# A kept-back stage prepared beside the last MLP, and an MLP bias on another engine

## What is computed

```python
# first block, B = 16 batches of 112 rows x 512 channels
out = attention(layer_norm(x, ln1), ctx) @ cproj_w + cproj_b
residual = out + x
y = gelu(layer_norm(residual, ln2) @ fc_w + fc_b, approximate=True) @ proj_w + proj_b
x = residual + y                                   # proj_b is the MLP bias
# second block: recurrence (time mixing), then channel mixing
x1 = x + group_norm(scan(r, k, v, w)) * g @ Wo.T
xc = _ln(x1, ln2_w, ln2_b)
sx2 = concatenate([state[:, 0:1] - xc[:, :1], xc[:, :-1] - xc[:, 1:]], axis=1)
xk2 = xc + sx2 * ffn_maa_k
xr2 = xc + sx2 * ffn_maa_r
rr = sigmoid(xr2 @ Wfr.T)
kk = square(relu(xk2 @ Wfk.T))
return x1 + rr * (kk @ Wfv.T)
```

## Time and profile before

| what | value |
|---|---|
| median of 3 executions | 1761.23 us (1757.83 to 1768.81) |
| the profiled execution | 1756.24 us, span 1753.9 us |
| PE busy | 1638.1 us (93%) |
| DVE busy | 1188.7 us (68%) |
| ACT busy | 657.4 us (37%) |
| POOL busy | 281.6 us (16%) |
| mean granted clock of TensorE | 0.975 |

### The profile page before, as it was taken

How to read it: one execution, slowest core, us unless ns; L and a number is a source line. 1 busy time by engine, 2 the same in 40 slices (tenths; PEclk the granted TensorE clock), 3 DMA queues, 4 the chain that set the end, 5 groups by cost and what they waited for, 6 DMA issues and landing times.

```text
span 1753.9 us, 21083 instructions
## 1 busy us (share of the span) xinstructions
PE 1638.1 (93%) x7912; PEld 855.8 (49%) x7912; DVE 1188.7 (68%) x1854; ACT 657.4 (37%) x1535; POOL 281.6 (16%) x377
## 2 busy tenths in 40 slices
PE   6999999799999999899999998999899898987968
PEld 3555544455555444455554445555444454433423
DVE  1233200367997995569988955799899576999741
ACT  2466420226664212246662222466431226212111
POOL 1100000123111001322110011221100132036020
PEclk9999999899999999999999999999999998999989
DMA  8001012143121124341112233510132343232221
GB/s 272 6 30 53 19 48 80 68 138 99 38 61 50 64 84 143 102 135 46 38 59 75 76 129 96 161 46 9 47 101 83 117 115 111 64 105 77 69 90 45
DMA packets 76914, 142.46 MB, mean 81 GB/s; under 512 B 16688, under 2 KB 26800, under 8 KB 76816
## 3 DMA queue, kind: packets, MB, share of 16 engines
q1 hardware_dynamic: 61664, 105.51, 18.9%
q0 software_dynamic: 11776, 31.70, 6.4%
q10 hardware_dynamic: 3376, 3.93, 0.7%
HBM read 117.26 MB, written 23.86 MB: 80 GB/s over the span
## 4 chain that ended last, share of the span: by engine, by line
PE 74%; DVE 16%; issue 4%; ACT 3%; ACTq 1%; DMA 1%; POOL 0%; DVEq 0%; POOLq 0%
PE bank L346 42%; PE bank L533 12%; PE bank L660 7%; PE bank L388 4%; DVE C L1399 3%; PE bank L380 3%; PE bank L400 2%; DVE sm L1336 1%; PE bank L626 1%; DVE C L1575 1%; DVE C L1391 1%; PE bank L611 1%; DVE SX L1399 1%; DVE C L1408 1%; DVE YB L1417 1%
## 5 line engine op out<-in xcount | busy, mean ns | idle before, releaser
L1399 DVE TENSOR_TENSOR_SCAN C<-XA,C 128x896 f32<-128x896 f32 x112 | 228.8, 2043 | 3.7 <-ACT XA L1091 0.5
L533 PE MATMUL bank<-ring,HT 128*112 128x512 f32 x512 | 222.3, 592 | 0.0
L1336 DVE CUSTOM_DVE_ANT_0 sm<-bank,maskb 112x375 f32<-112x375 f32 x256 | 124.3, 543 | 133.6 <-PE bank L380 133.1
L346 PE MATMUL bank<-ctx_t,Wk 128*128 128x375 f32 x512 | 195.2, 506 | 13.9 <-DMA Wk<-in_wk 12.5
L346 PE MATMUL bank<-SX,ring 128*128 128x448 f32 (+2 forms) x544 | 195.9, 519 | 4.1 <-issue 4.1
L346 PE MATMUL bank<-Wv,ctx_t 128*125 128x512 f32 x384 | 180.9, 596 | 0.4 <-ACT C L1057 0.4
L388 PEld LDWEIGHTS bank<-ident,sm 112*125 112x125 f32 x768 | 124.1, 190 | 105.6 <-ACT sm L1072 44.1
L1078 ACT ACTIVATE probT<-bank 125x336 f32<-125x336 f32 x256 | 114.3, 446 | 159.3 <-PE bank L388 157.6
L1072 ACT ACTIVATE sm<-sm,nm 112x375 f32<-112x375 f32 x256 | 153.4, 599 | 2.7 <-DVE nm L1336 2.7
L533 PEld LDWEIGHTS bank<-ring,HT 128*112 128x112 f32 x512 | 90.6, 177 | 127.2 <-issue 127.2
L346 PEld LDWEIGHTS bank<-SX,ring 128*128 128x128 f32 x544 | 100.5, 190 | 96.9 <-issue 94.0
(11 more groups left out here) (181 smaller groups left out, 2317.1 us busy)
## 6 DMA issues: line engine op xcount, KB each, us to landing
ring<-in_stream SPq DMA_DIRECT2D x64, 1024.0 KB, 5.4
ctx_t<-in_ctxT SPq DMA_DIRECT2D x16, 750.0 KB, 4.7
rkw_scratch<-HT POOLq DMA_DIRECT2D x32, 224.0 KB, 4.3
rkw<-rkw_scratch POOLq DMA_DIRECT2D x24, 224.0 KB, 3.1
HT<-in_x SPq DMA_DIRECT2D x16, 224.0 KB, 5.2
X<-in_x SPq DMA_DIRECT2D x16, 224.0 KB, 5.1
rkw_scratch<-YB POOLq DMA_DIRECT2D x16, 224.0 KB, 3.1
v_scratch<-HT POOLq DMA_DIRECT2D x16, 224.0 KB, 5.6
```

The source lines that it names most:

```text
L346: last_ = nc.tensor.matmul(out_ap, pairs[k][0], pairs[k][1], start=(k == 0), stop=(k == len(pairs) - 1))
L533: last_ = nc.tensor.matmul(bank[SC[b]][0:LQ, :], HT[:, c, b * LQ:(b + 1) * LQ], w[:, c, :], start=(m == 0 and c == 0), stop=(m == 3 and c ...
L1336: nc.vector.tensor_tensor_reduce(out=sm[0:LQ, slot, :], in0=tile(name)[0:LQ, 0:LK], in1=maskb[:, n % 2, :], scale=-SCALE, scalar=3.0e38, o ...
L1399: own.step(nc.vector.tensor_tensor_scan(out=part, data0=wrep[:, i % 2, :], data1=part, initial=0.0, op0=ALU.mult, op1=ALU.add))
```

## The change

Three things change.

1. `LAST` becomes 0, 2, 1, 3: stage 0 now handles group 0 and stage 1 handles group 2. Rows of groups 0 and 1 are both loaded from DRAM into `sm`.
2. The preparation of stage 0 moves from `pre(3)` into the last MLP: `last_stats(0)` behind the first whole iteration of the scan that runs there, `last_std(0)` on POOL at the same place, `last_norm(0)` on ACT one batch behind each GELU of quarter m = 0, the transposes between the first projection and the second FC, the columns behind the fourth normalisation, and `last_mixes(0)` between `group_norm` and `gate`. At the end of `pre(3)`, `last_mixes(1)` takes its place ahead of the last scan; on ACT and PE the columns of stage 1 stand between the second and the third tile of the gate product.
3. `mlp_bias` goes from DVE to POOL: four adds of one batch each, and `mlp_add` waits for them.

```diff
-LAST = [2, 0, 1, 3]
+LAST = [0, 2, 1, 3]
...
-            return x1_b[b] if LAST[k] == 0 else X[:, GB * (LAST[k] == NG - 1) + b, :]
+            return x1_b[b] if LAST[k] < 2 else X[:, GB * (LAST[k] == NG - 1) + b, :]
...  (tensor, mlp)
                     else:
                         piece_done(g, ("pj", m))
+                    if g == NG - 1 and m == 0:
+                        last_cols(0)
...  (tensor, pre)
-                if g == NG - 1:
-                    last_cols(0)
                 if g != NG - 2:
-                    w, late = weights(g, PRE_P[3]), g < NG - 1
+                    w, names = weights(g, PRE_P[3]), [("P", g, 4, e) for e in range(E)]
                     pe.wait_ge(mix_ready, g * MIXES + MIXED[4])
-                    channels_out([("P", g, 4, e) for e in range(E)], w, mixed[4], any_bank, hi=E - late)
-                    if not late:
+                    if g < NG - 1:
+                        channels_out(names, w, mixed[4], any_bank, hi=E - 1)
+                    else:
+                        channels_out(names, w, mixed[4], any_bank, hi=2)
+                        last_cols(1)
+                        channels_out(names, w, mixed[4], any_bank, lo=2)
                         piece_done(g, PRE_P[3])
-                if g == NG - 1:
-                    last_cols(1)
...  (gpsimd)
                     inv_std("ln2", g * GB + GB)
-                    if g > 0:
+                    for b in range(GB):
+                        pool.wait_ge(xn_ready["ln2"], g * GB + GB)
+                        nc.gpsimd.tensor_tensor(rows_of(g, b), rows_of(g, b), pb[:, :], ALU.add).then_inc(bias_added, 1)
+                    if g == NG - 1:
+                        blocks_after(p, IN_STEPS, IN_STEPS + UNITS)
+                        last_std(0)
+                        blocks_after(p, IN_STEPS + UNITS, RS * UNITS)
+                    elif g > 0:
                         blocks_after(p, IN_STEPS, RS * UNITS)
...
-                if g == NG - 1:
-                    last_std(0)
                 pool.wait_ge(w_out, 64 * (g + 1))
...  (scalar, mlp, behind the GELU)
+                        if g == NG - 1 and m == 0:
+                            last_norm(0, e, e + 1)
+                            if e == E - 1:
+                                last_cols(0)
...  (scalar, pre)
                 if g == NG - 1:
-                    last_norm(0)
-                    last_cols(0)
+                    last_norm(1)
                 for e in range(0 if g == NG - 2 else E - (g < NG - 1)):
+                    if g == NG - 1 and e == 2:
+                        last_cols(1)
                     name = ("P", g, 4, e)
                     ready(act, name)
                     nc.scalar.activation(GT[:, e, :], tile(name)[:, 0:T], ACT.Silu).then_inc(freed(name), 1)
-                if g == NG - 1:
-                    last_norm(1)
-                    last_cols(1)
...  (vector)
             def last_stats(k):
-                if 0 < k < NG - 1:
-                    dve.wait_ge(x1_in, 64 * k)
+                if LAST[k] < 2:
+                    dve.wait_ge(x1_in, 64 * (LAST[k] + 1))
...
             def mlp_add(g, b):
                 name, rows = ("ACC", g, b), rows_of(g, b)
                 ready(dve, name)
+                dve.wait_ge(bias_added, g * GB + b + 1)
...
                     if g == NG - 1 and j == 2:
-                        last_stats(0)
                         last_stats(1)
                 if g == NG - 1:
-                    last_mixes(0)
+                    last_mixes(1)
...
                     y_apply(n)
-                    mlp_bias(g)
-                    if g > 0:
+                    if g == NG - 1:
+                        units(p, IN_STEPS, IN_STEPS + UNITS)
+                        last_stats(0)
+                        units(p, IN_STEPS + UNITS, RS * UNITS)
+                    elif g > 0:
                         units(p, IN_STEPS, RS * UNITS)
                     if g > 0:
                         group_norm(p)
+                        if g == NG - 1:
+                            last_mixes(0)
                         gate(g)
...  (vector, last scan)
                     for i in range(RS):
-                        if i == 2:
-                            last_mixes(1)
-                        elif i in (7, 8):
+                        if i in (7, 8):
```

More of the change, by code:

```diff
@@ L257, in build @@
         mlp_used = sem("mlp_used")
+        bias_added = sem("bias_added")
         x1_out, x1_in = sem("x1_out"), sem("x1_in")
@@ L823, in _ @@
                     for b in range(GB):
-                        load_x1(1, b)
+                        load_x1(0, b)
                 if g < NG:
@@ L1172, in pre_cols, with last_norm @@
                     cols_out(("LN", "pre", g, b), lambda e: XA[:, e, b, 1:LQ + 1], "r_ln1_w", "r_ln1_b")
-            def last_norm(k):
-                for b in range(GB):
+            def last_norm(k, lo=0, hi=GB):
+                for b in range(lo, hi):
                     act.wait_ge(shift_ready, k * GB + b + 1)
@@ L1523, in gate @@
                 nc.vector.tensor_tensor(C[0][:, :, :], C[0][:, :, :], GT[:, :, :], ALU.mult).then_inc(og_ready, 1)
[L1525 to L1529, removed]
             def mlp_add(g, b):
```

## The result

| | before | changed |
|---|---|---|
| median, 20 executions each | 1762.28 us (1756.72 to 1768.81) | 1756.60 us (1749.44 to 1763.22) |
| ratio, 95% interval | | 0.9971 [0.9959, 0.9983] |
| profiled execution | 1756.24 us, clock 0.975 | 1754.84 us, span 1752.7, clock 0.978 |

The change is a gain of 0.3%, some 5 us, where I forecast a loss of 3.8 us. The profiled execution of before lies 6 us under its median, so the two profiles are nearly alike in time; they are compared stage by stage, from the first FC matmul of the last MLP (1273.8 us before, 1273.0 now).

A forecast was written before the change was run, and what follows sets the result against it. The chain ran through PE in the last MLP and border, ACT's columns, then DVE's last scan. D 8.9 + 2.1 in front of the scan - 7.2 in it = +3.8 us: 1760.0 profiled, 1765 median, range 1756 to 1772.

The forecast's parts named there:

- the time of GpSimd's shifts: Last MLP: the shifts of stage 0's four blocks end 2.3, 5.3, 11.9 and 18.1 us after the statistics start.
- D: Time by which PE leaves the last MLP's first quarter later, delaying what follows; predicted 8.9 us, bounds 4 and 12.
- the lower bound of 4: D if the shifts came in steps of 3.0 us, with waits only for the second GELU and the last bank.
- the second GELU: Last MLP, first quarter: held in ACT's queue, it ends at 1291.0 where PE's projection wants it at 1289.5; 1.5 us lost.
- the fourth: Last MLP, first quarter: the fourth GELU, held behind a shift, ends at 1300.6 and costs PE's projection 2.7 us.
- The clock loss of 1.6 us: PE's granted clock falls behind the gaps in the first quarter; one such loss is not hidden and adds 1.6 us to D.
- The bias on GpSimd: Scan iteration beside the adds takes 3.93 us more, DVE saves 2.29; the net 1.6 us per MLP is hidden, costed at zero.
- The work on DVE: Last MLP: mixing of 7.2 us fits DVE's 9.18 us wait for y; the gate is early if D is above 2.4.
- In front of the scan: Ahead of the last scan, two SiLUs and their table load delay the column write; scan starts 2.1 us later beside D.
- In the scan: Last scan: the second stage's mixing no longer stands between two iterations, -7.2 us.
- the rival on PE: PE becomes what the last scan waits for, its first sum at a lower clock; +10 to +13 us, about 1773; chance 0.10.
- nearly free: GpSimd's small instructions slip between DVE's, D is 4 or 2; sum -1 to -3 us, 1758 to 1760; chance 0.22.

The follow-up runs named there:

- e9: The changed kernel with the statistics of stage 0 four DVE instructions later; 1763.78 us, ratio 1.0006 to the kernel before.
- e3: The kernel before with only the MLP bias moved to GpSimd; 1762.39 us, ratio 0.9998.
- e11: The changed kernel with the mixing of stage 1 inside the last scan and the bias back on DVE; 1744.56 us, ratio 0.9908 to the kernel before.
- e2: The changed kernel run again, unchanged, for a second profile; 1756.63 us, ratio 0.9974 to the kernel before.
- e12: The changed kernel with stage 1 mixed inside the last scan and stage 0 normalised and transposed one MLP quarter later; 1745.56 us, ratio 0.9898.
- e6: The changed kernel with normalisation and transposes of stage 0 one MLP quarter later; 1756.40 us, ratio 0.9960 to the kernel before.
- e10: The changed kernel with stage 1's columns ahead of all SiLUs on ACT and its transposes ahead of the receptance product on PE; 1756.29 us, ratio 0.9965.
- e5: The changed kernel with the mixing of stage 1 put between the second and third iteration of the last scan; 1741.35 us, ratio 0.9876 to before.
- e1: The kernel before run again, unchanged, for a second profile; 1764.69 us, ratio 1.0011.
- e8: The kernel before with only the order of the kept-back groups changed to 0, 2, 1; 1763.81 us, ratio 1.0005.
- e7: The changed kernel with stage 0's statistics ahead of the scan iteration and GpSimd's shifts ahead of its bias adds; 1758.55 us, ratio 0.9974 to before.

## Why the prediction was wrong

**The step that failed** is the time of GpSimd's shifts, and with it D: 3.4 us, not 8.9, and under the lower bound of 4 that I gave. The mechanism was right, that small GpSimd instructions wait for the end of the DVE instruction that runs, and e9 gives my numbers to 0.2 us where the sequence of DVE is that of the earlier trace rows. But I took the earlier trace rows over to a place where another sequence follows the statistics. The order of the changed kernel, which lay before me, shows a short product and a short sum there. Term by term: the second GELU cost 1.0 us where I had 1.5, the fourth nothing where I had 2.7, and what stands between the end of the projection and the next FC (the transposes 1.7, the bank 0.5) 2.2 where I had 3.1. The clock loss of 1.6 us that I had added didn't come: behind a gap of 1.0 us the clock stayed at 1.00. The lower bound of 4 rested on even steps of 3.0 us between the shifts. The steps were 1.4, 4.3 and 6.3.

**The bias on GpSimd.** Right: the iteration beside the adds took 14.73 us from its short product to the statistics (1270.64 to 1285.37) instead of 10.88 (1273.89 to 1284.77), +3.85 for a predicted +3.93, and groups 1 and 2 hid it (e3). In the last MLP it makes the statistics later, as I had counted, and that is 1.2 us of D (e11).

**The work on DVE.** Right: hidden in the wait for y, the gate early for a D above 2.4. In the changed kernel PE takes it 1.1 us after it is ready (0.1 us in e2, where y came later), and e12 and e6, with a D of 2.2, find that bound.

**In front of the scan.** Predicted +2.1. From the start of those 24 matmuls (see e10) it is +2.0 between the first two profiles (1.6 to 2.0 over all), and e10 takes 2.3 us back.

**In the scan.** Predicted -7.2, measured -7.3. The lower clock at PE's first sum came, as the rival on PE had it (5.65 us instead of 3.17, behind 13.61 us idle), but DVE did not wait for it: PE did not become the bound, and in e5 it followed a third iteration 15.6 us earlier.

**The sum.** With D at 3.4 the terms as measured give 3.4 + 2.0 - 7.3 = -1.9 us, "nearly free" among the rivals. The medians differ by 5.7 us and the ratio by 5.1, so 3 to 4 us are left over, for which I had no term. From the first FC of the last MLP to the end of the span it is 480.1 and 482.7 us in the two profiles of before, 479.7 and 479.6 in those of the changed kernel: a part of it may lie there, where the first profile of before was a fast one. The start of that FC varies more, from 1273.0 to 1281.5 us over the profiles of all kernels, so single profiles can't place the rest.

TensorE's granted clock goes with it. Its mean was 0.9723 over the 83 executions of before in the runs e1 to e12 and 0.9748 over 32 of the changed kernel (standard errors 0.0002 and 0.0003), and a line through either set falls by 1.3 to 1.4 us for each 0.001. Read from these lines at a clock of 0.975 the times are 1759.0 and 1757.0, 2.0 us apart. That is the sum, but it is no proof. The same line would give e5 some 6 us for its higher clock (0.9790 against e2's 0.9747) beside its 15.6 us of work, and the median fell by 15.3 in all. A lower clock beside an idle stretch is already in the stages' lengths, so the clock is not a term of its own between kernels. Nor does it go with the early preparation: e1 and e8, without it, have 0.9716 and 0.9715, but e9, with it, has 0.9725. The cause of the 3 to 4 us stays open, and only with them does the median, 1756.6, come to lie at the lower edge of the range of 1756 to 1772.

**The Trainium skill.** The rule on DVE and GpSimd in "SBUF — State Buffer", section "Who interferes with whom", says that a DVE instruction with two SBUF inputs contends with a GpSimd instruction that reads SBUF. The rows above agree for all small instructions that began under a 2 us instruction of DVE. The one of 1291.08 does not quite fit: by the profile it and the accumulation overlapped for 0.5 us and neither was longer (0.57 and 2.02 us). What I drew from it, a D near 9, was wrong: which DVE instructions run in those microseconds tells how often the rule bites. The other rival, "nearly free", had come out of leaving the rule away, and its number was right for another reason.

## What to carry to other kernels

Before a measured pattern of waits is taken over to another place, lay the two instruction sequences of the interfering engine side by side; whether a short or a long instruction followed decided here over 4 us of the last shift (14.2 or 18.3) and 3 us of the quarter. And when a change takes preparation out of a serial stretch, ask what is left there: the larger gain, 15 us, lay in letting the scan begin without the remaining preparation, which DVE's idle time ahead of the mixing had shown: 15.6 us in the changed kernel, and 13.6 already before (up to 1462.06). With engines in order, a step is moved past everything in its queue, the next block's load too (e7).

## What the runs showed of the hardware that I had not expected

- A GpSimd instruction of 0.22 to 0.57 us alone took 1.5 to 2.4 us where it began under one of DVE's 2 us instructions, and ended within 0.4 us of that one's end. Yet at 1291.08 one that began under DVE's 0.27 us sum kept its 0.57 us. Moving four DVE instructions ahead changed the last shift by 4.1 us (14.2 to 18.3).
- Beside GpSimd's adds DVE's product took 2.98 us instead of 2.02, and its short sum 1.33 instead of 0.27, about 1 us for each add. DVE's two scans of 2.04 us, behind the adds, kept their time.
- TensorE's mean granted clock differed between two kernels with the same matmuls in another order by 0.0025. Within one kernel the time falls by 1.3 to 1.4 us for each 0.001 of it, but between e2 and e5 that line failed: 0.0043 more, and no gain beyond the 15.6 us of work.
- The way of y through DRAM, from DVE's last product to the gate, took 8.9 to 10.6 us over the 14 profiles, and 9.2 and 10.1 in the two of the changed kernel.
